# First layer: the scan's weights are split at other experts, and in the last group the rows' transfers are queued ahead of the last two weight loads

## What is computed

```python
xn = layernorm(x)                       # rows of 256
x = x + attn0(xn) + ffn0(xn)            # first layer
xn = layernorm(x)
x = x + scan1(xn) + ffn1(xn)            # second layer
# attn0: q, k, v, gate projections; decayed products inside chunks of 32 rows; output projection; + xn
# ffn0:  out = sum over 16 experts e of sigmoid(xn . sel_e) * relu(xn @ keys_e) @ values_e
# scan1: per mixture m of 4: sigmoid(xn@Wg_m+bg) * tanh(xn@Wv_m+bv), a = 0.001+0.998*sigmoid(xn@Wd_m+bd),
#        h_t = a_t*h_(t-1) + x_t; the two best mixtures of a row are summed with softmax weights
# ffn1:  the one best of 8 experts per row: relu(xn @ w1_e + b1_e) @ w2_e + b2_e
```

## Time and profile before

| | us |
|---|---|
| median of 3 runs | 1040.9 (1040.36 to 1041.03) |
| the profiled execution | 1038.94 |
| its span, first to last instruction | 1037.1 |
| TensorE busy | 1023.9 |
| VectorE busy | 785.0 |
| ScalarE busy | 627.0 |
| GpSimd busy | 320.5 |

### The profile page before, as it was taken

One profiled execution on the slowest core, in us unless ns is written; L12 is line 12 of the kernel. 1 busy time (PEld: TensorE's weight loads), 2 busy tenths in 40 slices (PEclk: granted clock), 3 DMA queues, 4 the chain that ended last, 5 costly groups with the idle time before them and its releaser, 6 DMA issues. The chain is left out here.

```text
span 1037.1 us, 20069 instructions
## 1 busy us (share of the span) xinstructions
PE 1023.9 (99%) x6510; PEld 917.3 (88%) x6510; DVE 785.0 (76%) x1284; ACT 627.0 (60%) x1186; POOL 320.5 (31%) x284
## 2 busy tenths in 40 slices
PE   8999999999999999998999999999999999999998
PEld 7998989888898998887877888999999999888887
DVE  6876767667586777858779998876777777588887
ACT  4553445435354454544566666888888888566665
POOL 3343444444444444333542871000000000382000
PEclk9999999999999999999999999999999999999999
DMA  6236313222141322532446384587888776652203
GB/s 192 64 95 211 97 40 81 81 61 61 52 99 51 81 82 73 171 111 72 168 162 261 103 287 180 192 280 246 280 275 262 257 257 203 225 163 84 89 13 102
DMA packets 144114, 152.13 MB, mean 147 GB/s; under 512 B 69184, under 2 KB 114112, under 8 KB 143040
## 3 DMA queue, kind: packets, MB, share of 16 engines
q1 hardware_dynamic: 135296, 137.47, 41.4%
q0 software_dynamic: 3072, 8.39, 2.4%
q10 hardware_dynamic: 5696, 5.64, 1.7%
HBM read 109.20 MB, written 42.27 MB: 146 GB/s over the span
## 5 line engine op out<-in xcount | busy, mean ns | idle before, releaser
L806 POOL TENSOR_TENSOR acc<-acc,ytmp 128x512 f32<-128x512 f32 x120 | 158.1, 1317 | 250.2 <-ACT ytmp L897 230.5
L1637 ACT ACTIVATE act_o<-ps,scan_bias 128x512 f32<-128x512 f32 x189 | 129.8, 688 | 100.0 <-PE ps L393 95.8
L897 ACT ACTIVATE ytmp<-ps,sel 128x256 f32<-128x256 f32 x256 | 107.3, 470 | 100.3 <-PE ps L1175 100.0
L974 DVE SCALAR_TENSOR_TENSOR hT_l<-ps,hT_h 128x512 fp32r<-128x512 f32 (+1 forms) x136 | 88.3, 654 | 99.8 <-ACT hT_h L857 99.6
L1173 PE MATMUL ps<-vals_h,hT_h 128*128 128x256 f32 x512 | 145.6, 284 | 5.3 <-DVE hT_l L974 5.3
L1174 PE MATMUL ps<-vals_l,hT_h 128*128 128x256 f32 x512 | 144.4, 282 | 0.0
L1175 PE MATMUL ps<-vals_h,hT_l 128*128 128x256 f32 x512 | 144.1, 281 | 0.0
L857 ACT ACTIVATE hT_h<-ps 128x512 fp32r<-128x512 f32 x128 | 76.3, 596 | 88.5 <-PE ps L393 83.9
L1961 DVE TENSOR_TENSOR_SCAN h_b<-a_b,hstate,xs_b 128x512 f32<-128x512 f32 x63 | 88.0, 1396 | 30.4 <-ACT a_b L1644 27.1
L1173 PEld LDWEIGHTS ps<-vals_h,hT_h 128*128 128x128 f32 x512 | 96.9, 189 | 12.0 <-DVE hT_l L974 6.1
L1789 POOL DMA_INDIRECT late_y<-y_d,pos_i x20 | 23.1, 1154 | 272.3 <-DMA y_d<-y_sb 266.5
(11 more groups left out here) (261 smaller groups left out, 2769.9 us busy)
## 6 DMA issues: line engine op xcount, KB each, us to landing
raw<-w SPq DMA_DIRECT2D x78, 512.0 KB, 4.5
x1T<-xT_d SPq DMA_DIRECT2D x16, 512.0 KB, 5.3
comb_b<-comb_d SPq DMA_DIRECT2D x8, 1024.0 KB, 8.1
xn_d<-xn SPq DMA_DIRECT2D x15, 512.0 KB, 3.0
w_small<-w SPq DMA_DIRECT2D x14, 512.0 KB, 4.5
xs_d<-zeros ACTq DMA_DIRECT2D x1, 4992.0 KB, 19.8
x_d<-x SPq DMA_DIRECT2D x8, 512.0 KB, 4.2
xT_d<-nT_h SPq DMA_DIRECT2D x8, 512.0 KB, 2.7
```

The costliest lines, as they stand in the source:

```text
L806: pool.tensor_tensor(dst[:, 2:4, :], acc[:, 2:4, :], ytmp[:, k % 2, :, :], ALU.add).then_inc(acc23, 1)
L897: act.activation(ytmp[:, k % 2, j - 2, :], yb(k, j), ACT.Copy, scale=sel[:, j, k:k + 1]).then_inc(y_23, 1)
L974: dve.scalar_tensor_tensor(out=hT_l[:, k % 2, t], in0=ps[:, k % 2, t], scalar=0.0, in1=hT_h[:, k % 2, t].bitcast(F32), op0=ALU.max, op1=AL ...
L1637: act.activation(act_o[:, i % 2, w, :], ps[:, 3 * (i % 2) + w, :], func, bias=scan_bias[:, w, i:i + 1]).then_inc(act_g, 1)
```

## The change

The two tables of splits are altered. In group 6: l0 moves from k = 1 to 0, l1 from 3 to 1, l2 from 6 to 2, l3 from 7 to 2, l4 from 10 to 4; l5 stays at 11. In group 7: b00 from 1 to 0, b01 from 3 to 1, b02 from 6 to 2, b10 from 7 to 2, b11 from 10 to 5, b12 from 11 to 6. On SP only b00, b01, b02 and b10 are still loaded ahead of body(7); the loads of b11 and b12 stand behind it. The loads of l0 to l5 stay where they were.

```diff
@@ -681,8 +681,8 @@
-        LATE_SPLITS = {1: ["l0"], 3: ["l1"], 6: ["l2"], 7: ["l3"], 10: ["l4"], 11: ["l5"]}
-        LAST_SPLITS = {1: ["b00"], 3: ["b01"], 6: ["b02"], 7: ["b10"], 10: ["b11"], 11: ["b12"]}
+        LATE_SPLITS = {0: ["l0"], 1: ["l1"], 2: ["l2", "l3"], 4: ["l4"], 11: ["l5"]}
+        LAST_SPLITS = {0: ["b00"], 1: ["b01"], 2: ["b02", "b10"], 5: ["b11"], 6: ["b12"]}
@@ -755,9 +755,11 @@
-            for name in order[n_l:n_b]:
+            for name in order[n_l:n_l + N_STAGE]:
                 weight(name)
             body(GROUPS - 1, False, True)
+            for name in order[n_l + N_STAGE:n_b]:
+                weight(name)
             xT1_store(sp, GROUPS - 2)
```

## The result

The changed kernel takes 1054.7 us (median; 1054.0 to 1055.1), where the kernel before takes 1040.6 on the same terms: the ratio is 1.0137, with a 95% interval of 1.0124 to 1.015. Forecast were 1056.1 us and a range of 1051 to 1061. By the medians the change costs 14.1 us; forecast were 15.2. The profiled execution has a span of 1052.2 us, which is 15.1 more than before. Which profile of the kernel before one takes matters for that: a second one has a span of 1038.4 us, and then it is 13.8. That the total fits so well is partly luck.

The account below looks back on a forecast made before the run. TensorE's matmuls were taken as the bound. Stalls of 10.1 and 9.1 us, 1.7 us of slow clock behind each, less 7.4 regained, gave +15.2 us on the median 1040.9: 1056.1 us, range 1051 to 1061.

Parts of the forecast that it names:

- What bounds the kernel: Whole kernel: TensorE is busy 1023.9 of 1037.1 us, so only longer or shorter standing of TensorE matters.
- The split of l4: Group 6, k = 4: ACT and DVE wait for l4's late load; TensorE stalls 10.1 us (9.1 to 10.5) before expert 6's down product.
- The split of b11: Group 7, k = 5: b11 loads behind the quarter loads; TensorE stalls 9.1 us (7.1 to 10.1) before expert 7's down product.
- The clock: Behind each of the two new stalls: half-speed matmuls cost 1.7 us more, bounds 0 to 3.4.
- What the moves take away: Expert 9's down product, groups 6 and 7: without splits at k = 7, stalls and slow clock go, giving back 7.4 us.
- The sum: First layer: two stalls and their clock terms less the regained time, +15.2 us in all.
- The reordering: SP's loads in group 7: x1's store may go earlier, but quarter loads also wait for xn1's store, so no gain.
- (a): Loads of l4 and b11 land in time, no new stall, 7.4 us pure gain: 1033.5 us; chance 5%.
- (b): Only one stall comes, the last group being covered: 1045.3 us; chance 4%.
- (c): Stalls breed others through DVE's backlog and the clock stays low longer: 1062 to 1066 us; chance 9%.

Follow-up runs that it names:

- every chunk ready: Both tables of the change, but l4, b11 and b12 loaded early enough, against the kernel before: ratio 0.9984; a second run with ranks and top moved earlier: 0.9979.
- ranks ahead: Tables of the change, all chunks loaded early, ranks at k = 5, 6, 7 and mixture top at k = 7, against the kernel before: ratio 0.9979.
- normalisation early: Kernel before, with DVE's normalisation for the second layer at k = 2 and 3 instead of 3 and 4 in groups 6 and 7: ratio 0.9994.
- group 7 alone: Kernel before, with only group 7's table and SP's load order from the change: ratio 1.0041, on a chip with a disturbed scan stage.

## Why the prediction was right, point by point

**What bounds the kernel.** Right. Nothing but TensorE's standing time and its clock moved the end, and every run could be read from these.

**The split of l4.** The mechanism held in every link: l4 issued at 415.21 (forecast 415.3), DVE's normalisation 0.1 us late (0.2), no stall from two splits at k = 2. The stall was forecast as 10.1 us, within 9.1 to 10.5, and was 9.2. The term that was off is the landing: I took the 3.8 us of the earlier trace rows, and it took 3.1. The prediction's reason for a shorter one, the store of xn that ran beside it before and is late now, isn't borne out: in the ten profiles with that store right behind, the load issued at this place landed in 3.0 to 3.8 us (3.3 in the later profile of the kernel before), and in 3.0 and 3.1 in the two without. The 3.8 was the longest of them all, a single row taken for the rule.

**The split of b11.** Forecast 9.1 us, measured 7.2, the near end of the range. The quarter loads were issued in 4.06 us and not in 5.13, and the landing took 3.2 and not 3.8: together 1.7 of the 1.9 us. The rank piece cost 0.7 us, as assumed, not 1.65. What makes SP take 4.9 to 5.4 us in some profiles and 4.06 in others is not settled; in the kernel before, one of the eight issues took 1.56 us and the others at most 0.49.

**The clock.** Forecast 1.7 us behind each, measured 2.0 and 2.7. This term was too small by 1.3 us in all. It was the row behind a stall of 3.88 us, carried over to stalls of twice the length; what the clock does behind those stands at the end.

**What the moves take away.** For group 6 this step failed, and the total hides it. In the changed kernel the stalls at expert 9 are indeed gone, and all 7.4 us appear as regained. But I gave the split at k = 7 the credit. In group 6 the two runs with every chunk ready, which have no split there, keep 1.26 and 1.08 us of stall, and the one without splits at k = 2 to 7 keeps 0.79; in all three DVE stands for the quarter loads. In the changed kernel DVE doesn't stand for them; TensorE comes some 9 us later to expert 9, which gave these loads time. In group 7 the mechanism was right: in the first run with every chunk ready and in the one with group 7's table and the old order, the four rank operations ran while ACT made oT_h and hT_h, and DVE had no wait for the quarter loads. There 0.79 and 0.88 us stay, within the "up to 1 us" that I had allowed, but from sig_g, which comes late, and not from the ranks. My ground for group 6 was that groups 1 to 5 have no splits and no stall; they also have no collision of the normalisation with POOL, which is a second difference that I didn't look for.

**What is late next.** A stall of 1.7 us at expert 11 was not in the sum: DVE's last rank and the top stand in front of hT_l of expert 11, where the long stall at expert 9 had given DVE the time for them before. I had allowed up to 1 us for ranks, at expert 9.

**The sum.** 9.2 + 2.0 + 7.2 + 2.7 + 1.7 - 7.4 = +15.4 us measured (the ends of the first layer differ by 15.3), against 10.1 + 1.7 + 9.1 + 1.7 - 7.4 = +15.2 forecast. The two stalls were taken 2.8 us too long; the clock (1.3) and the missing stall (1.7) make up for that. The 7.4 us are those of one profile of the kernel before; in its later profile the stalls and the clock come to 1.6 us more.

**The reordering.** Right that it brings nothing by itself: 1.0004.

**Rivals.** (a), that the loads are in time, and (b), that only one stall comes, are refuted by ACT's two rows. (c), that the stalls breed others and the clock stays low longer, was right on the clock alone: the one more stall, at expert 11, is no child of the long ones, as it is there without them too (1.51 us in the first run with every chunk ready).

The Trainium skill, DMA: Bandwidth & Descriptors, section Anatomy of one DMA, says that waits are taken where a transfer is issued. The rows agree: l4's transfer was issued 0.05 us behind the last quarter load, at 415.21, while its buffer had been free since l0's split. Its fit gives 2.6 us for 256 KB, on another issuing path; measured were 3.1 and 3.2 behind the quarter loads, so an estimate by the page's figure would have been 0.5 to 0.6 us short, where mine was 0.6 to 0.7 long.

## What to carry to other kernels

Before a consumer is moved forward in a queue that runs in order, find when the transfer that it waits for is *issued*, and read the waits of the issuing queue ahead of it: here two splits went six and five steps forward while their loads stood behind eight others, and what stood behind them on ACT cost some 18 us of the first layer (508.9 to 527.0). When a stall is to be removed, look for a second cause that would come true just behind the first, and test it by a run that makes the first harmless. Where a total fits, check the terms: this forecast was right to 0.2%, with four of its terms wrong.

## What the runs showed of the hardware

A DVE operation of 0.40 us took 1.43 when POOL began an addition of 1.3 us as it started, and when the DVE pair came 0.1 us earlier, it kept its time and POOL's addition took 1.41 us. So in these pairs the one that began first kept its pace. What the two engines share, no run here shows. A rank operation of 0.2 us that began during a POOL addition took 1.21.

The granted clock fell behind shorter stalls than I had expected, and in the first layer the longer stalls go with longer stretches at 0.50. The whole stretches at 0.50 (columns as above, of PE alone), first for the kernel before in its later profile, at the stall of 4.20 us:

```profile
488.00:494.70 6.70, 5.66 (x20) 0.50 0.00 0
```

then for the changed kernel, at those of 9.01 and 7.03:

```profile
414.00:424.20 10.20, 3.90 (x15) 0.50 0.34 82
489.10:499.30 10.20, 5.34 (x25) 0.50 0.19 56
```

Over the first layer in all profiles named here: 3.4 us at the stalls of 1.81 us (l4 at k = 6), 2.33 (ranks ahead), 3.63 (normalisation early) and 3.88 (before, the first profile); 6.8 at those of 4.20 to 6.94; 10.2 at those of 7.02, 7.03, 8.95 and 9.01; none at those of 0.79 to 1.53. A part of the stretch falls into the stall and costs nothing: 6.3 of the 10.2 us at the stall of 9.01, which is why the longest stall paid less for the clock than that of 7.03. At the stalls of 1.81 and 2.33 it fell only 0.7 and 0.9 us after TensorE had restarted, and so all 3.4 us were paid at half speed: a stall of 2.33 us cost 4, where two of 0.79 and 1.51 cost their own length. The length of a stall does not settle it, though. In the scan's stage on the disturbed chip, one of 7.63 us (in the run with every chunk ready) had a stretch of 6.8 and not 10.2, and one of 2.74 (in the run with group 7 alone) had none.
